# Scores and row maxima of even and odd heads in two strips of TensorE's rows, with two-part products in the FFN's format

## The reference

```python
qkv = x @ c_attn_w + c_attn_b                       # x: 16 x 512 x 128
scores = einsum('bhqd,bhkd->bhqk', q, k) / sqrt(8)  # causal, 16 heads, hd = 8
attn = softmax(where(causal, scores, min))
# heads 0, 1, 2: attn times 1.6 in one third of the keys, renormalised
out = einsum('bhqk,bhkd->bhqd', attn, v) @ c_proj_w + c_proj_b
x = layernorm(x + out)
h = concat([x, -x]); h = s0 * (h @ sign(k0)); h = relu(h) * 2
h = s1 * (h @ sign(k1)); h = relu(h) * 2
x = layernorm(x + s2 * (h @ sign(k2)))
```

## Time and profile before

| | us |
|---|---|
| median of 3 runs | 921.8 |
| lowest, highest | 920.85, 927.9 |
| the profiled execution's own time | 922.26 |
| its span, first to last instruction | 919.5 |
| mean granted TensorE clock | 0.964 of full speed |

### The profile page before, as it was taken

One profiled execution on the slowest core, in us unless ns is written; L12 is line 12 of the kernel. 1 busy time (PEld: TensorE's weight loads), 2 busy tenths in 40 slices (PEclk: granted clock), 3 DMA queues, 4 the chain that ended last, 5 costly groups with the idle time before them and its releaser, 6 DMA issues.

```text
span 919.5 us, 17053 instructions
## 1 busy us (share of the span) xinstructions
PE 835.0 (91%) x5696; PEld 427.4 (46%) x5696; DVE 621.4 (68%) x2617; ACT 608.3 (66%) x1091; POOL 527.3 (57%) x763
## 2 busy tenths in 40 slices
PE   4488599999999999999999999999999999999875
PEld 1133244545455554545454554545454554545353
DVE  3487386685958587685858587685869587774124
ACT  3036267686776777676776777677776778586743
POOL 4215146575756657575756657575756658384732
PEclk9669699999999999999999999999999999999988
DMA  5735545545353545545352545545353535300000
GB/s 106 87 46 66 65 57 63 68 48 86 42 81 45 74 50 74 67 49 91 36 83 44 74 51 76 63 49 85 45 81 45 77 39 75 50 14 13 24 1 23
DMA packets 65741, 53.16 MB, mean 58 GB/s; under 512 B 5015, under 2 KB 63351, under 8 KB 65655
## 3 DMA queue, kind: packets, MB, share of 16 engines
q1 hardware_dynamic: 63542, 49.72, 39.7%
q0 software_dynamic: 960, 1.58, 1.4%
q10 hardware_dynamic: 1152, 0.79, 0.6%
HBM read 9.24 MB, written 4.19 MB: 15 GB/s over the span
## 4 chain that ended last, share of the span: by engine, by line
PE 60%; DVE 13%; ACT 7%; POOL 7%; issue 7%; DMA 5%; SPq 1%; POOLq 0%; DVEq 0%; ACTq 0%
PE av_ps L1005 11%; PE max_ps L946 11%; PE bank_ps L1032 9%; PE score_ps L970 8%; PE bank_ps L1033 7%; DVE max_ps L774 7%; PE bank_ps L929 4%; POOL res L549 3%; PE bank_ps L1080 3%; DMA stack<-parts 2%; ACT full L633 2%; ACT e L641 2%; DMA stack<-rowmaxT 2%; PE bank_ps L1047 2%; POOL rstd L539 2%
## 5 line engine op out<-in xcount | busy, mean ns | idle before, releaser
L774 DVE CUSTOM_DVE_ANT_0 max_ps<-max_ps,future 128x512 f32<-128x512 f32 (+3 forms) x1024 | 477.6, 517 | 233.9 <-PE max_ps L946 230.4
L641 ACT ACTIVATE e<-score_ps 128x512 f32<-128x512 f32 x640 | 371.3, 613 | 255.9 <-PE score_ps L970 254.6
L946 PE MATMUL max_ps<-stack 72*128 72x512 bf16 (+3 forms) x1024 | 247.6, 312 | 20.8 <-DMA stack<-parts 12.8
L970 PE MATMUL score_ps<-stack 75*128 75x512 bf16 (+3 forms) x1024 | 244.1, 303 | 17.6 <-DMA stack<-rowmaxT 10.6
L511 POOL TENSOR_SCALAR_AFFINE_SELECT e<-e 128x512 f32<-128x512 f32 x256 | 160.1, 637 | 172.2 <-ACT e L641 172.0
L519 POOL TENSOR_TENSOR h_lo<-full,h_hi 128x512 fp32r<-128x512 f32 x119 | 151.5, 1278 | 84.0 <-ACT full L633 83.9
L1005 PE MATMUL av_ps<-e,vaug 128*25 128x512 f32 (+3 forms) x2048 | 191.3, 447 | 0.0
L946 PEld LDWEIGHTS max_ps<-stack 72*128 72x128 bf16 x1024 | 81.3, 99 | 156.5 <-issue 94.0
L774 DVE DVE_READ_ACCUMULATOR2_ANT rowmax<- 128x1 f32 x1024 | 143.8, 140 | 0.0
L970 PEld LDWEIGHTS score_ps<-stack 75*128 75x128 bf16 x1024 | 91.2, 98 | 91.5 <-ACT e L641 35.0
L1032 PE MATMUL bank_ps<-h_hi,w 128*128 128x512 f32 x256 | 109.6, 428 | 0.4 <-DVE h_lo L854 0.4
(11 more groups left out here) (95 smaller groups left out, 725.8 us busy)
## 6 DMA issues: line engine op xcount, KB each, us to landing
stack<-parts SPq DMA_DIRECT2D x276, 128.0 KB
x_in<-in_L_attn_hidden_states SPq DMA_DIRECT2D x16, 256.0 KB, 15.2
x_res<-in_L_attn_hidden_states SPq DMA_DIRECT2D x16, 256.0 KB, 2.9
out_x<-res SPq DMA_DIRECT2D x16, 256.0 KB, 3.4
stack<-parts POOLq DMA_DIRECT2D x12, 128.0 KB, 12.9
stack<-rowmaxT ACTq DMA_DIRECT2D x32, 24.0 KB
e<-in_L_ffn_k SPq DMA_DIRECT2D x1, 256.0 KB, 3.3
e<-in_L_attn_c_attn_w SPq DMA_DIRECT2D x1, 128.0 KB, 2.9
```

The lines of the kernel that those rows point to most:

```text
L641: nc.scalar.activation(e[g % 2][:, t, :], score_ps[:, t % 2, :], ACT.Exp, scale=SCALE).then_inc(exped, 1)
L774: return nc.vector.tensor_tensor_reduce(out=scored_block, in0=scored_block, in1=future[:, P * (T - 1 - qt):S], scale=1.0, scalar=NEG, op0= ...
L946: return nc.tensor.matmul(out_ap[:, col:col + width], st[0:QK_ROWS, h, 0, P * qt:P * qt + P], st[0:QK_ROWS, h, 1, 0:width], start=True, st ...
L970: return nc.tensor.matmul(out_ap[:, col:col + width], st[0:ALL_ROWS, h, 1, P * kt:P * kt + P], st[0:ALL_ROWS, h, 0, P * kt:S], start=True, ...
```

## The change

- `stack` has 8 slots instead of 16, in float32r instead of bf16. Even heads lie in rows 0 to 34, odd heads in rows 64 to 98 (`ROW_TILE` 64). q and k are split into two float32r parts, so 4 products of 8 features give 32 rows (`QK_ROWS`), and 35 with the maximum's three.
- `max_scores` and `scores` are generators that stop after each product; `in_turn` issues one product of each alternately. `MAX_ORDER` sets the maxima's order so that the maximum's heads and the scores' heads of a step lie in different strips.
- The middle part's instructions are gone on ScalarE and GpSimd (lines 716 and one of 494 and 496), `qk` too: the second part is written in place in `parts`.
- 8 copies a half instead of 9, of the same 128 KB, each from 32 partitions in rows of 2 KB instead of 64 partitions in rows of 1 KB. GpSimd issues 10 for batch 0, and SP 6.
- `rowmaxT` is 24 rows of the FFN's `x1_lo`, float32r instead of bf16; its DMA is two for each half. Two waits guard the shared memory: VectorE's copy of half 0 waits for `ffn0_3` of the batch before, and the low part of x1 waits for the row maxima's DMA of half 1.

The diff, cut to its core (renamed indices, the same edit for constants, and semaphore counts that follow from the number of copies are left out):

```diff
-MIDDLE_STEP = (1, 0)
 MAX_TWICE = ((0, 1), (0, 3), (0, 5))
+MAX_IN_FRONT = len(MAX_TWICE)
-COPIES_OF_POOL = ((1, 0), (1, 1), (0, 2), (2, 0), (2, 1), (2, 2))
+COPIES = tuple((a, c, odd) for a in range(2) for c in range(2) for odd in range(2))
+COPIES_OF_POOL = ((0, 0, 1), (0, 1, 1), (1, 0, 1), (1, 1, 0), (1, 1, 1))
-    QK_ROWS, MAX_ROW = 72, 72
-    ALL_ROWS = MAX_ROW + 3
+    ROW_TILE, QK_ROWS = 64, 32
+    ALL_ROWS = QK_ROWS + 3
+    def kinds(half, odd):
+        return [(half, odd, t) for t in range(STEPS)]
+    MAX_ORDER = (kinds(0, 1)[:MAX_IN_FRONT] + kinds(0, 0) + kinds(0, 1)[MAX_IN_FRONT:]
+                 + kinds(1, 0) + kinds(1, 1))
-        stack = [sb(f"stack{i}", [P, H, 2, S], BF16) for i in range(2)]
+        stack = [sb(f"stack{i}", [P, HALF, 2, S], F32R) for i in range(2)]
-        qk = sb("qk", [P, 2, S])
-        parts = [sb(f"parts{i}", [P, 6, S], BF16) for i in range(2)]
+        parts = [sb(f"parts{i}", [P, 4, S], F32R) for i in range(2)]
-        rowmaxT = sb("rowmaxT", [3 * HALF, S], BF16)
+        rowmaxT = x1_lo[0:3 * HALF, :]
+        def copy(eng, b, half, a, c, odd):
+            row = ROW_TILE * odd + R * (2 * a + c)
+            col = 64 * half + 32 * odd
+            return eng.dma_start(stack[b.parity][row:row + R, G * half:G * half + G, :, :].bitcast(F32),
+                                 parts[b.parity][col:col + 32, a:c + 3:c + 2 - a, :].bitcast(F32))
+                for a, c, odd in COPIES:
+                    if (a + c == 0) in high and (a, c, odd) not in pool_does:
+                        copy(sp, b, half, a, c, odd).then_inc(stacked[b.parity][half], 16)
 # GpSimd
-                if k == 0:
-                    ins = nc.gpsimd.tensor_tensor(qk[:], qk[:], pt[:, 0:4:3, :], ALU.subtract)
-                else:
-                    ins = nc.gpsimd.tensor_tensor(pt[:, 2:6:3, :], qk[:], pt[:, 1:5:3, :], ALU.subtract)
+                nc.gpsimd.tensor_tensor(pt[:, 1:4:2, :], pt[:, 1:4:2, :].bitcast(F32), pt[:, 0:4:2, :].bitcast(F32),
+                                        ALU.subtract).then_inc(split_step, 1)
 # ScalarE
-                nc.scalar.dma_start(stack[b.parity][MAX_ROW:ALL_ROWS, HALF * half:HALF * half + HALF, 0, :],
-                                    rowmaxT[:]).then_inc(rowmax_in[half], 16)
+                for odd in range(2):
+                    row = ROW_TILE * odd
+                    nc.scalar.dma_start(stack[b.parity][row + QK_ROWS:row + ALL_ROWS, G * half:G * half + G, 0, :]
+                                        .bitcast(F32), rowmaxT[3 * G * odd:3 * G * odd + 3 * G, :].bitcast(F32)
+                                        ).then_inc(rowmax_in[half], 16)
-                            nc.scalar.activation(parts[n.parity][:, 1:5:3, :], qk[:], ACT.Copy).then_inc(split_step, 1)
 # VectorE
+                if not half and live(b + -2):
+                    wait_full(dve, use_of(b + -2, "ffn0_3"))
+                                if live(n):
+                                    dve.wait_ge(rowmax_in[1], n.times(32, 32))
 # TensorE
+            def max_scores(b, i):
+                half, odd, t = MAX_ORDER[i]
+                row = ROW_TILE * odd
+                def part(j, qt, col):
+                    width = P * (qt + 1)
+                    slot = G * half + j
+                    return nc.tensor.matmul(out_ap[:, col:col + width],
+                                            st[row:row + QK_ROWS, slot, 0, P * qt:P * qt + P],
+                                            st[row:row + QK_ROWS, slot, 1, 0:width], start=True, stop=True)
                 if t < 4:
-                    last = part(G * g + t, 3, 0)
+                    last = part(t, 3, 0)
                 elif t < 8:
-                    part(G * g + t - 4, 2, 0)
-                    last = part(G * g + t - 4, 0, 3 * P)
+                    part(t - 4, 2, 0)
+                    yield
+                    last = part(t - 4, 0, 3 * P)
 ...
+            def in_turn(*programs):
+                for _ in zip_longest(*programs):
+                    pass
-                        for b, quarter, step in max_steps(n, g, t):
-                            max_scores(b, quarter, step)
-                        if live(n):
-                            scores(n, g, t)
+                        steps = list(max_steps(n, g, t))
+                        for b, i in steps[:-1]:
+                            in_turn(max_scores(b, i))
+                        in_turn(*[max_scores(b, i) for b, i in steps[-1:]], *[scores(n, g, t) for _ in range(live(n))])
```

More of the change, by code:

```diff
@@ L24 @@
 from contextlib import ExitStack
+from itertools import zip_longest
 import concourse.bass as bass
@@ L522, in split_rowmax @@
             def split_rowmax(b, half):
[L524 to L525 removed]
+                m, r = (z[:, half].rearrange("p t (o h) -> p t o h", o=2) for z in (rowmax, rowmax_rest))
+                hi, mid, lo = (rowmax_parts[:, half, :, :, i, :] for i in range(3))
                 pool.wait_ge(max_taken, b.times(G * STEPS, 2 * STEPS * (half + 1)))
@@ L859, in iteration @@
                     for t in range(STEPS):
-                        for b, quarter, step in max_steps(n, g, t):
-                            take_max(b, quarter, step)
+                        for b, i in max_steps(n, g, t):
+                            take_max(b, i)
                         for what, d, _, step in places(n):
@@ L930, in transposes @@
                 last.then_inc(bank_full[u[0]], 1)
-            def max_scores(b, g, t):
-                i = STEPS * g + t
-                st, out_ap = stack[b.parity], max_ps[:, i % MAX_RING, :]
-                if t == 0 and g % 2 == 0:
-                    wait_stacked(pe, b, g // 2)
-                last_use = i - MAX_RING
-                if i < MAX_RING:
-                    last_use = max(j - G * STEPS for j in range(G * STEPS) if j % MAX_RING == i)
-                if not (b.c == 0 and last_use < 0):
-                    pe.wait_ge(max_taken, b.times(G * STEPS, last_use + 1))
-                def part(h, qt, col):
+            def max_scores(b, i):
+                half, odd, t = MAX_ORDER[i]
+                row = ROW_TILE * odd
+                st, out_ap = stack[b.parity], max_ps[:, b.times(G * STEPS, i) % MAX_RING, :]
+                if i % (2 * STEPS) == 0:
+                    wait_stacked(pe, b, half)
+                if b.times(G * STEPS, i) >= MAX_RING:
+                    pe.wait_ge(max_taken, b.times(G * STEPS, i + 1 - MAX_RING))
+                def part(j, qt, col):
```

171 lines of the change are left out of this document (72 added, 99 removed).

## The result

The changed kernel takes 1819.5 us (median of 4 runs, 1803.3 to 1849.7) where the kernel before took 922.3 beside it: ratio 1.965, 95% interval 1.947 to 1.982. It is almost twice as slow. The profiled execution is the slowest of the four, 1849.7 us; its span is 1846.7 us.

What follows compares the result with a forecast made beforehand. TensorE, VectorE and ScalarE bound by turns, TensorE for some 23.6 of 51.6 us an iteration. 14 x (-3.3 + 0.9 + 0.2) = -31 us, with the start -35, takes 922.3 to 887 us; range 860 to 945.

Steps and rivals of the forecast that it cites:

- What bounded the kernel: Steady iteration of 51.6 us: TensorE, VectorE and ScalarE bound it by turns, TensorE for some 23.6 us in 15 steps.
- Pairs overlap at 0.22 us gained: Maximum's and score's products in two row strips: a pair costs 0.23 us instead of 0.45, 3.3 us an iteration.
- The rival of two shapes: Rival: maxima and scores are two array shapes and each alternation empties the array; 1070 us or more, chance 0.15.
- The clock, under 3 in 100: TensorE's granted clock: a rival given under 3 in 100, since with pairs TensorE streams over 70% of the second stretch.
- Loads side by side: Weight loads of different row strips run together; were they in turn, the gain would be 1.1 us an iteration.
- Excursions, 0.08 each, once: Some 11 full-array groups inside TensorE's 15 steps leave the strips, 0.08 us each, 0.9 us an iteration.
- Narrow products at the streamed price: Products below 512 columns in the new format cost by streamed columns, 0.06 us for 128, not 0.25.
- Other engines and DMA at 0: Removed GpSimd and ScalarE work, VectorE's new waits and the DMAs change nothing; only VectorE's copy adds 0.2 us an iteration.
- Start, a gain of 4 us: Before the first maximum: subtractions, a ScalarE pass and 2 of 18 copies go, some 4 us gained, bounds 0 and 8.
- The range: Whole kernel: 860 to 945 us, leaving out the two shapes and the tips of the other rivals, 0.19.

Runs made afterwards that it cites:

- e1: Products on TensorE alone, the whole computation left out, in ten stages of different row counts, widths and formats between full-array products; it ran 252 us.
- e2: The changed kernel with one more row of zeros in each strip, so 33 and 36 rows of one shape; 1041.5 us.
- e5: Products on TensorE alone, the computation left out, in seven stages of 35 to 72 rows, pairs with full-array products, and alternation; no total time given.
- e6: The changed kernel with 29 more rows of zeros in each strip, so 61 and 64 rows; 985.2 us, ratio 1.068.
- e9: e6 with the strips taken away, products over full-array rows, zeroing shared by two engines, part of the computation changed; 956.9 us, ratio 1.036.

## Why the prediction was wrong, step by step

**What bounded the kernel.** The reading itself holds; it was TensorE, VectorE and ScalarE by turns. It carried little weight, since the new cost is so large that TensorE bounds all three stretches (110.00 us busy in the 110 from 860 to 970 us).

**Pairs overlap at 0.22 us gained.** True for strips of one shape (e1 B, C, J; e2), and wrong for the kernel as changed, whose two strips have 32 and 35 rows. This is the step that failed. The forecast took "strips" from the column strips of line 1005, which are all of one shape, and carried that to two that aren't. In place of a pair in 0.23 us the runs show each of the two products 0.42 us after the other (e1 A), and in place of an iteration of 49.4 us one of 108.7.

**The rival of two shapes.** It named the mechanism, the rows (32 against 64) and the signs to look for: starts over 0.3 us apart (0.42 at full clock) and TensorE bounding the second stretch. It had a chance of 0.15 and a time of "1070 or more". Against it stood one row, the change to the column strips at 0.08. That row held only half of the price: leaving a shape costs 0.10 there too, but in the FFN's format the first product behind the change costs 0.11 more, and between 32 and 35 rows every product is a first one. In bf16, the format of the scores in the kernel before, that second half isn't seen (0.10 in all). The trace of before has the missing row, just behind those of the earlier trace rows, where an FFN product follows the column strips:

```profile
407.42 0.50 PE L1032 MATMUL bank_ps<-x_hi,w 128*128 128x512 f32 x1
407.76 0.40 PE L1033 MATMUL bank_ps<-x_lo,w 128*128 128x512 f32 x1
408.00 0.39 PE L946 MATMUL max_ps<-stack 72*128 72x512 bf16 x1
```

0.34 us for the first, 0.24 for the second. The rival's sum was off as well: its own prices, 0.08 and 0.16 a change, give 16 x 0.16 + 24 x 0.32 = 10 us an iteration and twice that, 20, so the 14 that it called the low end isn't it. With all changes counted and none hidden, shapes alone would give, by the estimate above, 922 + 16 x 15 to 21 = 1160 to 1260 us. The rest, up to 1850, is the clock.

**The clock, under 3 in 100.** The second term that failed. The prediction reasoned from how much of the time TensorE streams, and expected no fall as pairs stream more. The runs show two other things: the clock fell in products of 35 or 48 rows in one strip even without a gap (e1 D, e5 A and B), and it also fell in streams of changes of shape, though the busy share reads 100% (e1 A and I, e5 G). The alternation of 32 and 35 rows has both, and no run tells their shares apart. A busy share of 98% on the page was no sign of a fast engine.

The page "TensorE: Matmul & The Clock Gate" of the Trainium skill (Part 1) ties the lower rate to an idle TensorE. For a gapless strip of 35 rows the runs don't agree with that.

**Loads side by side.** Right: a pair of 128-column products in 0.11 us (e1 E), where a single one in the full array takes 0.11 as well (F).

**Excursions, 0.08 each, once.** Mis-sized. One costs some 0.4 us (e5 E): 0.10 for each way and 0.11 for what comes first behind each change. The upper bound that the prediction gave was 0.16. It also counted only the 11 in TensorE's stretches. In all there are some 59 changes in and out, against 32 in the kernel before. This takes the gain of overlap away even in e6: overlap saves at most 40 x 0.22 = 8.8 us an iteration, but TensorE is busy 813.2 / 16 = 50.8 us an iteration in e6, and 819.7 / 16 = 51.2 in e9, which has the same format and no strips; before it was 777.3 / 16 = 48.6. So rows of zeros alone didn't mend the change.

The page "TensorEngine Tiling (Array Packing)" of the Trainium skill (Key Properties) had the rule that a change of tiling mode drains the engine. The runs agree, and put 0.10 us on it, and 0.11 on the first product behind it in this format.

**Narrow products at the streamed price.** Right where the loads have cover: in e6 a 128-column pair that stands behind another is followed after 0.06 us (498.50 to 498.56). Several in a row take 0.11 each, the distance of their loads (e1 E, F).

**Other engines and DMA at 0.** Right for the copies: they land after 6.9 to 18.0 us (6.2 to 18.6 before). TensorE waits 6.5 us in all for them. Of VectorE's copy and its new waits nothing is to be seen beside 1040 us of waiting for maxima.

**Start, a gain of 4 us.** Wrong in sign. After, SP's queue and the first maximum:

```profile
7.26 5.52 SPq L376 DMA_DIRECT2D stack<-e  x4
...
35.79 0.79 PE L936 MATMUL max_ps<-stack 32*128 32x512 f32 x1 [6.49 <-DMA stack<-parts]
```

The first maximum starts at 35.79 us, before at 33.21. The rows of ones for the maximum are now four DMAs instead of two, one for each strip of each stack, and take SP 5.52 us to issue. The loads and copies behind them on that queue are late by as much as the subtractions saved and more. The prediction's list of the DMAs had left these out. That they are the cause of the 2.6 us was read from the queue, not tried.

**The range.** 860 to 945 left the two shapes outside on purpose. The fault lies ahead of it. A rule that speaks against the change was at hand, the rows of the change (32 and 35) met its condition, and the only row against it held half of the price.

## What to carry to other kernels

Give all row strips that shall run together the same shape, if need be by rows of zeros: one row of zeros was worth 780 us here. Before using strips, count the changes of shape that they bring, those around the neighbours' full-array products too, at 0.1 to 0.2 us each way; with some 40 pairs an iteration that gain 0.22 us each, 59 changes used up the gain. Before calling a rival unlikely by a row's price, look in the same trace for a row in the format that the change will use, and price the product behind the change too. Read the granted clock next to the busy share.

## What the runs showed of the hardware

- Row strips of 32 and of 35 rows in turn don't overlap: 0.20 us more for each product in the FFN's format at full clock, 0.29 at half, 0.10 in bf16. Strips of 32/32, 35/35, 33/36 and 61/64 rows run together.
- A change between row strips, column strips and the full array costs 0.09 to 0.10 us, and the first 512-column product behind it in the FFN's format 0.11 more (0.34 instead of 0.23 in e5 E and before). An excursion of two full-array products between pairs costs some 0.4 us.
- Two strips' weight loads take the time of one (0.11 us for a pair of 128-column products), and four strips of 32 rows take 0.23 us for four products of 512 columns.
- The granted clock fell to 0.50 in gapless products of 35 or 48 rows in one strip, and stayed at 1.00 with 64 rows in one strip or 72 in the full array. It stayed at 1.00 in e5 E too, pairs of 36 rows and full-array products in turn.
- In the kernel, 61/64 instead of 33/36 rows with the same products took the clock from 0.865 to 0.906 and 4.3 us from an iteration. Why the stretches of e5 (E, F) show no such difference stays open.
